# Two half projections begun one step earlier in an attention kernel's hand-written order of steps

## The chip, the cores and the metric

The kernel runs on one core of a Trainium2 chip. The metric is the device time of one execution in microseconds (us), lower is better.

## The reference

Two layers on x of 8 batches, 512 channels and 1024 positions, in float32. Only the first is touched:

```python
h = _group_norm(x, gn_w, gn_b)
qkv = jnp.einsum('oc,bcn->bon', qkv_w, h.reshape(B, C, N)) + qkv_b[None, :, None]
q, k, v = qkv.reshape(B, 3, NUM_HEADS, HEAD_DIM, N) split along axis 1
attn = softmax(jnp.einsum('bhdi,bhdj->bhij', q, k) * HEAD_DIM ** (-0.5))
out = jnp.einsum('bhij,bhdj->bhdi', attn, v)
x = x + (jnp.einsum('oc,bcn->bon', proj_w, out) + proj_b)
```

There are 8 heads of 64 channels. The second layer (a top-k attention over tokens) follows it on the same core.

## The kernel before

The first layer works through 64 heads in 32 pairs, four pairs to a batch. A head is 8 **steps**, so a pair is 16 steps, numbered 0 to 15 here; a step takes 256 keys against 512 queries. What each engine does in a step is written out by hand, and every engine runs its own list in order, waiting on semaphores.

- **PE** (`step`, L478): the second half of the weighting of an earlier step (`weigh_low`, L474, reads `p_low`); the scores, four matmuls (L447, L451); one matmul of 512 columns for the row maxima of three steps later (`take_max`, L428); then the **units** of this step; the weighting (L467, L468); a second maximum (L428). That is 12 matmuls without a unit.
- A **unit** is one half (512 positions) of a projection k, q or v of the *next* pair, a transposition of v, or a small group sum `g`. Most projections are spread: six matmuls (L372 to L374) in one step and six in the next. `PAIR_STEPS` (L52) gives, for each of the four pairs of a batch, the step in which each half begins; `parts_by_step` (L58) makes the table that all engines follow.
- **ACT** takes two exponentials of the scores, and the high part of a finished unit (L575 for q and k).
- **DVE** (`step`, L799): the reduce of the second maximum of the step before (L679); after every fourth block `row_max_top` (L687); `p_low` of the step before (L695), which frees a score tile; the reduce of this step's first maximum (L679); the low part of the units finished in the step before (L708 for q and k, two instructions); then what belongs to single steps: statistics of the next batch's x (`tile_stats`, L780 to L783, in a batch's second pair at steps 9, 11, 12 and 13), `h_low` (L787), `o_low` (L792, step 8), `reciprocal` (L797).
- **POOL** normalises a head's output (L878), when SP's transfer of the reciprocals has landed.
- **SP** issues the transfers of a step in order: copies of a finished k or q (`twins`, L938), the row of maxima (L943), the denominators (L950), weights, and in a fourth pair, at step 2, four loads of x for the residual (L980).

The maxima and units share three PSUM banks. `assign_banks` (L178) gives each one the bank that its own estimate says comes free first, and `fill_free` (L333) makes PE wait until what last had that bank has been read: by the reduce (L679) for a maximum, by the low part (L708) for q and k. So the order of units also decides which bank waits for which reduce.

Of the kernel before, what the change touches and what calls it, by code (L numbers as in the profile page):

```python
# [46 lines left out]
def begins(k0, k1, q0, q1, v0, v1, vt0, vt1, whole=()):  # L47
    begin = {("k", 0): k0, ("k", 1): k1, ("q", 0): q0, ("q", 1): q1, ("v", 0): v0, ("v", 1): v1}
    return {**{u: (s, u in whole) for u, s in begin.items()}, ("vt", 0): vt0, ("vt", 1): vt1}


PAIR_STEPS = (begins(0, 1, 6, 8, 2, 3, 3, 5, whole=(("k", 0), ("k", 1), ("v", 0), ("q", 1))),  # L52
              begins(1, 3, 5, 8, 10, 12, 12, 14),
              begins(0, 3, 6, 8, 10, 12, 12, 14),
              begins(2, 4, 6, 8, 10, 12, 12, 14))


def parts_by_step():  # L58
# [1996 lines left out]
```

## Time and profile before

| | us |
|---|---|
| median of three runs | 2720.56 |
| the three runs | 2714.07, 2722.04, 2720.56 |
| profiled execution, span | 2718.4 |
| PE busy in it | 2619.7 |
| DVE busy | 2055.1 |
| ACT busy | 1578.5 |
| POOL busy | 221.9 |

The span runs from the first to the last instruction of the profiled execution; the page gives no other time of that execution, and the time around the span is not in it. Busy time of PE is modelled at the ends of matmuls, so PE's losses are read below from start to start of the same instruction. Batches are counted from the first to the eighth; "the fifth batch" begins at 1139 us or so of the span.

### The profile page before, as it was taken

Reading aid. Unit: us, or ns where it says so; the run is one execution under the profiler, and the core shown is the slowest. Engines: PE = TensorE matmul, PEld = TensorE weight load, DVE = VectorE, ACT = ScalarE, POOL = GpSimd, SP = SyncE. Lnnn points to the kernel's source line nnn. Section 1 sums busy time; section 2 is a strip of 40 time slices with the busy share of each in tenths; the row PEclk is TensorE's granted clock in tenths of the full one; section 3 lists DMA queues with packets and bytes.
Section 4 is the critical chain, followed back from the end, with each engine's and each line's share of the span. In section 5 each row is a group of like instructions: output and inputs, shape, how many; then the busy total and the mean of one; then the engine's idle time right before and its main releaser. Section 6 shows DMA issues by size and latency. Waiting matters only on the chain.

```text
span 2718.4 us, 33180 instructions
## 1 busy us (share of the span) xinstructions
PE 2619.7 (96%) x11856; PEld 2181.7 (80%) x11856; DVE 2055.1 (76%) x3294; ACT 1578.5 (58%) x1930; POOL 221.9 (8%) x134
## 2 busy tenths in 40 slices
PE   6999999999999999999999999999999987899998
PEld 5788888888888888888888888888888876688887
DVE  6788768876887688768876887688767867878864
ACT  4667646764676467646764676567646663334311
POOL 1000000000000000000000000000000012111010
PEclk9999999999999999999999999999999999899999
DMA  4512232223222322232223222321322335466444
GB/s 156 177 50 80 67 103 61 79 71 100 64 78 67 101 67 76 63 107 67 65 72 109 66 59 79 109 67 48 90 83 58 112 127 203 171 215 246 165 164 170
DMA packets 154849, 279.48 MB, mean 103 GB/s; under 512 B 51776, under 2 KB 52032, under 8 KB 154176
## 3 DMA queue, kind: packets, MB, share of 16 engines
q1 hardware_dynamic: 152128, 268.98, 31.4%
q0 software_dynamic: 2560, 8.39, 1.0%
q8 instruction: 96, 1.57, 0.2%
q14 instruction: 65, 0.53, 0.1%
HBM read 180.04 MB, written 63.18 MB: 89 GB/s over the span
## 4 chain that ended last, share of the span: by engine, by line
PE 83%; DVE 9%; issue 3%; DMA 2%; ACT 1%; SPq 0%; POOL 0%; POOLq 0%; DVEq 0%; ACTq 0%
PE tiles L372 9%; PE tiles L373 8%; PE tiles L374 8%; PE tiles L474 8%; PE tiles L451 8%; PE tiles L428 8%; PE tiles L468 8%; PE tiles L467 8%; PE tiles L447 7%; PE tiles L1321 5%; PE tiles L1371 2%; DVE row_max L679 2%; DVE p_low L695 2%; DVE h_low L787 1%; PE tiles L383 1%
## 5 line engine op out<-in xcount | busy, mean ns | idle before, releaser
L679 DVE TENSOR_REDUCE row_max<-tiles 128x1 f32<-128x512 f32 x1014 | 694.5, 685 | 443.4 <-PE tiles L428 440.6
L544 ACT ACTIVATE p_high<-tiles 128x1024 fp32r<-128x1024 f32 x512 | 525.5, 1026 | 595.8 <-PE tiles L451 595.1
L695 DVE TENSOR_TENSOR p_low<-tiles,p_high 128x1024 fp32r<-128x1024 f32 x512 | 623.0, 1217 | 7.0 <-ACT tiles L546 6.2
L546 ACT ACTIVATE tiles<-tiles 128x1024 f32<-128x1024 f32 x512 | 523.0, 1021 | 0.0
L467 PE MATMUL tiles<-p_high,v_high 128*128 128x512 f32 x1024 | 406.5, 397 | 2.2 <-ACT num_den L562 1.5
L428 PE MATMUL tiles<-k_high_low,q_high_high 128*128 128x512 f32 x1014 | 404.8, 399 | 0.2 <-DVE row_max L679 0.2
L468 PE MATMUL tiles<-p_high,v_low 128*128 128x512 f32 x1024 | 402.0, 393 | 0.0
L428 PEld LDWEIGHTS tiles<-k_high_low,q_high_high 128*128 128x128 f32 x1014 | 312.5, 308 | 48.6 <-DVE row_max L679 5.7
L474 PE MATMUL tiles<-p_low,v_high 128*128 128x512 f32 x1024 | 325.8, 400 | 14.9 <-DVE p_low L695 14.6
L451 PE MATMUL tiles<-q_low_max,k_high_one 65*128 65x512 f32 x1024 | 325.8, 399 | 1.9 <-DMA q_low_max<-row_max_top 1.8
L372 PE MATMUL tiles<-h_high,w_high 128*128 128x512 f32 x768 | 304.6, 397 | 17.3 <-DVE row_max L679 8.3
L878 POOL TENSOR_TENSOR o_normed<-num_den,o_normed 64x1024 f32<-64x1024 f32 x64 | 153.5, 2399 | 2046.1 <-DMA o_normed<-rec_rows 2046.1
L447 PE MATMUL tiles<-q_high_high,k_high_low 128*128 128x512 f32 x1024 | 316.8, 391 | 0.0
L373 PE MATMUL tiles<-h_low,w_high 128*128 128x512 f32 x768 | 301.7, 393 | 0.0
L374 PE MATMUL tiles<-h_high,w_low 128*128 128x512 f32 x768 | 300.4, 391 | 0.0
L447 PEld LDWEIGHTS tiles<-q_high_high,k_high_low 128*128 128x128 f32 x1024 | 192.0, 188 | 47.6
L451 PEld LDWEIGHTS tiles<-q_low_max,k_high_one 65*128 65x128 f32 x1024 | 193.2, 189 | 45.6 <-DMA q_low_max<-row_max_top 4.4
L474 PEld LDWEIGHTS tiles<-p_low,v_high 128*128 128x128 f32 x1024 | 189.7, 188 | 44.9 <-DVE p_low L695 25.2
L467 PEld LDWEIGHTS tiles<-p_high,v_high 128*128 128x128 f32 x1024 | 192.5, 188 | 38.8 <-ACT num_den L562 2.3
L468 PEld LDWEIGHTS tiles<-p_high,v_low 128*128 128x128 f32 x1024 | 192.6, 188 | 38.0
L372 PEld LDWEIGHTS tiles<-h_high,w_high 128*128 128x128 f32 x768 | 145.8, 190 | 43.9 <-issue 24.2
L374 PEld LDWEIGHTS tiles<-h_high,w_low 128*128 128x128 f32 x768 | 145.1, 189 | 32.4
(167 smaller groups left out, 3138.1 us busy)
## 6 DMA issues: line engine op xcount, KB each, us to landing
x_tiles<-in_x SPq DMA_DIRECT2D x64, 512.0 KB, 5.4
w_high<-w_split SPq DMA_DIRECT2D x126, 256.0 KB, 2.8
w_low<-w_split SPq DMA_DIRECT2D x126, 256.0 KB, 3.0
k_high_one<-k_high_low SPq DMA_DIRECT2D x128, 128.0 KB, 2.3
q_high_high<-q_high_high SPq DMA_DIRECT2D x128, 128.0 KB, 2.3
o_normed<-rec_rows SPq DMA_DIRECT2D x64, 256.0 KB, 3.7
x<-x_tiles SPq DMA_DIRECT2D x32, 512.0 KB, 4.0
x_full<-x SPq DMA_DIRECT2D x32, 512.0 KB, 8.3
```

Of the source, the lines that this page charges most:

```text
L372: mm(fill[:, :], w1, high[:, c, cols], start=(c == 0), stop=False)
L374: last = mm(fill[:, :], w2, high[:, c, cols], start=False, stop=(c == CT - 1))
L428: mm(max_bank(h, i, n)[:, :], q1[:, q_slot(h), first:first + HALF - 3:4], k1[:, k_slot(h), n * HALF:(n + 1) * HALF], start=True, stop=True ...
L447: mm(out[:, n * HALF:(n + 1) * HALF], k1[:, wk, keys[n]], q1[:, wq, queries], start=True, stop=False)
L451: last = mm(out[:, n * HALF:(n + 1) * HALF], k2[0:HD + 1, wk, keys[n]], q2[0:HD + 1, wq, queries], start=False, stop=True)
L467: mm(pv[:, :], weights_of(v1, t, n), p, start=(t % 4 == 0 and n == 0), stop=False)
L468: last = mm(pv[:, :], weights_of(v2, t, n), p, start=False, stop=False)
L474: last = mm(pv[:, :], weights_of(v1, t, n), pl[:, t % 2, n * HALF:(n + 1) * HALF], start=False, stop=(t % 4 == 3 and n == 1))
L544: nc.scalar.activation(ph[:, r, :], ring[:, r, :], ACT.Exp, scale=ATT_SCALE).then_inc(s_ph, 1)
L546: nc.scalar.activation(ring[:, r, :], ring[:, r, :], ACT.Exp, scale=ATT_SCALE).then_inc(s_p32, 1)
L679: nc.vector.reduce_max(mcol[:, h % 2, n, i:i + 1], max_bank(h, i, n)[:, :], AX_X).then_inc(s_mx, 1)
L695: tt(pl[:, r, :], ring[:, r, :], ph[:, r, :].bitcast(F32), ALU.subtract).then_inc(s_pl, 1)
```

## The change

In the table for a batch's second pair, q's second half begins at step 7 instead of 8; in the fourth pair k's first half begins at step 1 instead of 2. Both are spread over two steps, so the six matmuls of step 9 (second pair) are now in step 7, and the six of step 3 (fourth pair) in step 1. The low part on DVE, the high part on ACT and the copies on SP move one step forward with them.

```diff
 PAIR_STEPS = (begins(0, 1, 6, 8, 2, 3, 3, 5, whole=(("k", 0), ("k", 1), ("v", 0), ("q", 1))),
-              begins(1, 3, 5, 8, 10, 12, 12, 14),
+              begins(1, 3, 5, 7, 10, 12, 12, 14),
               begins(0, 3, 6, 8, 10, 12, 12, 14),
-              begins(2, 4, 6, 8, 10, 12, 12, 14))
+              begins(1, 4, 6, 8, 10, 12, 12, 14))
```

The arguments of `begins` are the steps of k's two halves, q's two, v's two and the two transpositions. The seven fourth pairs that have a successor and the eight second pairs are changed.

DVE in a second pair, from the reduce of step 9's first maximum on, before (`bn_parts` and `mean_var` are the statistics of x, `q_low_max` is q's low part):

```order
L679 TENSOR_REDUCE row_max<-tiles 128x1
L780 BN_STATS bn_parts<-x_tiles 128x6 x2
L782 MEMSET carry 128x1
L783 BN_AGGR mean_var<-bn_parts 128x2
L679 TENSOR_REDUCE row_max<-tiles 128x1
L695 TENSOR_TENSOR p_low<-tiles,p_high 128x1024
L679 TENSOR_REDUCE row_max<-tiles 128x1
L708 SCALAR_TENSOR_TENSOR q_low_max<-tiles,bias_qk,q_high_high 64x512 x2
```

The same place after the change:

```order
L679 TENSOR_REDUCE row_max<-tiles 128x1
L708 SCALAR_TENSOR_TENSOR q_low_max<-tiles,bias_qk,q_high_high 64x512 x2
L780 BN_STATS bn_parts<-x_tiles 128x6 x2
L782 MEMSET carry 128x1
L783 BN_AGGR mean_var<-bn_parts 128x2
L679 TENSOR_REDUCE row_max<-tiles 128x1
L695 TENSOR_TENSOR p_low<-tiles,p_high 128x1024
```

q's low part now stands ahead of the statistics and of the reduce of step 9's second maximum.

SP in a fourth pair, around step 2 (`k_high_one` are k's copies, `q_low_max<-row_max_top` is the row of maxima):

```order
-L943 DMA q_low_max<-row_max_top 1x128x4 x2
+L943 DMA q_low_max<-row_max_top 1x128x4
+L938 DMA k_high_one<-k_high_low 64x512 x2
+L943 DMA q_low_max<-row_max_top 1x128x4
 L950 DMA den_columns<-num_den 128x1x8
 L980 DMA x_tiles<-in_x 128x1024 x4
-L938 DMA k_high_one<-k_high_low 64x512 x2
 L958 DMA rec_rows<-rec_columns 128x8
```

k's two copies stood behind the four loads of x, and now stand ahead of the row of maxima and the denominators.

PE in a third pair, at step 3, with the semaphores it waits on (`s_mx` counts reduces, `s_kql` low parts of k and q):

```order
 L451 MATMUL tiles<-q_low_max,k_high_one 128x512 x2
-L428 MATMUL tiles<-k_high_low,q_high_high 128x512 [waits s_kql]
-L372 MATMUL tiles<-h_high,w_high 128x512 [waits s_mx,s_w1]
+L428 MATMUL tiles<-k_high_low,q_high_high 128x512 [waits s_mx]
+L372 MATMUL tiles<-h_high,w_high 128x512 [waits s_kql,s_w1]
 L373 MATMUL tiles<-h_low,w_high 128x512
```

No instruction moves here; the two have exchanged their banks.

## Rows read from the trace of the kernel before

**Rows 1.** The page's busy times: engine, us, share of the span, instructions.

```profile
PE 2619.7 (96%) x11856; PEld 2181.7 (80%) x11856; DVE 2055.1 (76%) x3294; ACT 1578.5 (58%) x1930; POOL 221.9 (8%) x134
```

**Rows 2.** PE's waits over the span: waiter, releaser, us in total, times, longest.

```profile
PE tiles L474 <- DVE p_low L695: 14.6, 24, 1.7
...
PE tiles L372 <- DVE row_max L679: 8.3, 11, 1.0
```

**Rows 3.** Windows (us, busy by engine, PEclk, DMA), fifth batch: full, bare, fourth pair's 0, 1.

```profile
1249.45:1253.60 4.15, 4.15 (x20) 3.48 (x19) 3.82 (x8) 3.61 (x5) 0.00 (x0) 1.00 0.00 0
1400.72:1403.50 2.78, 2.78 (x13) 2.35 (x12) 2.75 (x5) 2.01 (x3) 0.00 (x0) 1.00 0.03 1
1339.89:1343.78 3.89, 3.38 (x13) 2.35 (x12) 3.89 (x6) 3.89 (x5) 0.00 (x0) 1.00 0.00 0
1343.78:1347.23 3.45, 3.05 (x13) 2.35 (x12) 3.45 (x5) 2.74 (x4) 0.00 (x0) 1.00 0.00 0
```

**Rows 4.** Windows, second pair's steps 7 and 8: fourth, fifth, last of eight batches, sum.

```profile
967.94:975.66 7.72, 7.46 (x32) 5.73 (x31) 7.55 (x11) 5.06 (x6) 2.40 (x1) 1.00 0.16 34
1240.96:1249.45 8.49, 7.48 (x31) 5.76 (x30) 8.30 (x11) 5.05 (x6) 1.35 (x1) 1.00 0.14 31
...
2062.93:2072.39 9.46, 7.47 (x31) 5.82 (x30) 9.29 (x11) 5.06 (x6) 2.35 (x1) 1.00 0.13 28
sum 68.74, PE 59.87 PEld 46.16 DVE 67.33 ACT 40.48 POOL 13.55; mean PE 7.48 PEld 5.77 DVE 8.42 ACT 5.06 POOL 1.69
```

**Rows 5.** Windows, fourth pair's steps 0 and 1: sum of seven batches.

```profile
sum 51.43, PE 45.05 PEld 32.88 DVE 51.43 ACT 46.38 POOL 0.00; mean PE 6.44 PEld 4.70 DVE 7.35 ACT 6.63 POOL 0.00
```

**Rows 6.** PE's timeline, fifth batch, second pair's step 8: start, us, what, [idle <-releaser].

```profile
1246.36 0.47 PE L372 MATMUL tiles<-h_high,w_high 128*128 128x512 f32 x1 [0.93 <-DVE row_max L679]
```

**Rows 7.** Line L687: ns min/median/max of one, first and last start.

```profile
L687 DVE TENSOR_TENSOR row_max_top<-row_max x128: 161/162/1917, 43.3 to 2199.1; 128x4 fp32r<-128x4 f32 x128
```

**Rows 8.** POOL's timeline, fifth batch, second pair's steps 6 and 7.

```profile
1239.92 2.40 POOL L878 TENSOR_TENSOR o_normed<-num_den,o_normed 64x1024 f32<-64x1024 f32 x1 [37.76 <-DMA o_normed<-rec_rows]
```

**Rows 9.** DVE's timeline, fifth batch, second pair's steps 7 to 9.

```profile
1241.41 0.92 DVE L687 TENSOR_TENSOR row_max_top<-row_max 128x4 fp32r<-128x4 f32 x1
...
1243.99 1.50 DVE L708 SCALAR_TENSOR_TENSOR q_low_max<-tiles,bias_qk,q_high_high 64x512 fp32r<-64x512 f32 x2
...
1247.86 1.22 DVE L792 TENSOR_TENSOR o_low<-o_normed,o_high 128x1024 fp32r<-128x1024 f32 x1
1249.18 0.69 DVE L679 TENSOR_REDUCE row_max<-tiles 128x1 f32<-128x512 f32 x1
...
1250.92 0.68 DVE L679 TENSOR_REDUCE row_max<-tiles 128x1 f32<-128x512 f32 x1
1251.52 1.28 DVE L780 BATCH_NORM_STATS2 bn_parts<-x_tiles 128x6 f32<-128x512 f32 x2
1252.84 0.20 DVE L783 BATCH_NORM_AGGREGATE mean_var<-bn_parts 128x2 f32<-128x12 f32 x1
```

**Rows 10.** PE's and DVE's timelines, fifth batch, third pair's step 3.

```profile
1289.02 0.40 PE L428 MATMUL tiles<-k_high_low,q_high_high 128*128 128x512 f32 x1
1289.52 0.47 PE L372 MATMUL tiles<-h_high,w_high 128*128 128x512 f32 x1
...
1288.68 0.69 DVE L679 TENSOR_REDUCE row_max<-tiles 128x1 f32<-128x512 f32 x1
```

**Rows 11.** DVE's timeline, fifth batch, fourth pair: last `h_low`, and step 3's reciprocal.

```profile
1347.12 1.22 DVE L787 TENSOR_TENSOR h_low<-x_tiles,h_high 128x1024 fp32r<-128x1024 f32 x1
...
1354.69 0.20 DVE L797 RECIPROCAL rec_columns<-den_columns 128x8 f32<-128x8 f32 x1 [0.92 <-DMA den_columns<-num_den]
```

**Rows 12.** SP's timeline, fifth batch: second pair's step 7, fourth pair's step 3.

```profile
1241.19 1.11 SPq L938 DMA_DIRECT2D q_high_high<-q_high_high  x2
...
1352.59 0.60 SPq L950 DMA_DIRECT2D den_columns<-num_den  x1
```

**Rows 13.** The page's transfers: KB of one, median us from issue to landing.

```profile
x_tiles<-in_x SPq DMA_DIRECT2D x64, 512.0 KB, 5.4
```

## Prediction

> **What bounds the kernel now.** I read first the page's busy shares: TensorE (PE) is busy 96% of the span, VectorE (DVE) 76% [rows 1]. So time is lost only where PE stands still, and the list of PE's own waits tells where: 14.6 us for `p_low`, which frees the score tiles, and 8.3 us for `row_max`, which frees a PSUM bank; both are DVE's work [rows 2]. Then I cut the first layer into its steps, from one pair of L447 matmuls to the next. A step holds 12 matmuls, or 18 with half a projection. A window over an undisturbed full step lasts 4.15 us, over an undisturbed bare one 2.78 us, both at granted clock 1.00 [rows 3]. What a step lasts beyond that is its loss, and the change touches two places that lose. In a second pair the bare step 7 and the full step 8 should take 6.93 us. They take 7.72 to 9.46; over eight batches 68.74 against 55.4, **13.3 us lost** [rows 4]. In a fourth pair the bare steps 0 and 1 should take 5.56 us and take 3.89 + 3.45 [rows 3]; over seven batches 51.43 against 38.9, **12.5 us** [rows 5]. All of both would be 25.8 us, 0.9% of the span; the question is what comes back where the bare step is put.
>
> All durations are from the profiled execution, whose span is 2718.4 us. Nothing gives its own time apart from the span; the median of the three runs is 2720.56, 2.2 us above the span, and I add the change to the median. A measurement here can tell about 0.3%, 8.2 us, from no change.
>
> **The second pair: no work is added, the bare step goes from 7 to 9.** I work in the fifth batch, where step 7 begins at 1240.96. Before, the half in step 8 takes the bank of the maximum that PE has just written at the end of bare step 7. Its reduce comes behind the rest of DVE's queue, and PE starts L372 only at 1246.36 [rows 6]. That goes: with a full step 7 the half uses an older bank, already read.
>
> But DVE's queue is not shortened. It opens with `row_max_top`, 0.92 us long from 1241.41, where the median of its 128 is 0.162 us [rows 7, 9]; it ends as the 2.40 us POOL operation from 1239.92 ends, at 1242.32 [rows 8]. **The Trainium skill**, "SBUF — State Buffer", section "Who interferes with whom", says that a DVE instruction with both inputs in SBUF waits for a GpSimd one that reads SBUF, and for its whole length; by that rule the trace agrees. The change moves neither operation, so the hold stays. Were nothing ever held, every batch would be like the fourth, and by the step below the sum of this place would be some 8 us in place of 4.
>
> From there DVE works without a gap to the end of `o_low` (1247.86 + 1.22 = 1249.08) [rows 9], before and after alike. After, step 9 starts at 1240.96 + 2 x 4.15 = 1249.26 and is bare; step 10 starts at 1252.05, and its half of v follows five matmuls of 0.23 us (2.78 / 12), at 1253.21. That half takes the bank of the maximum written at the end of step 9, now as before. DVE's queue in front of this reduce: the reduce of step 8 at 1249.08; step 9's first reduce 1.74 later (1249.18 to 1250.92 in the rows) at 1250.82; then, 0.60 later, q's low part, 1.50 us, which stood one step further on; then the group statistics, 1251.52 to 1253.04 in the rows, 1.52 us [rows 9]. That is 1254.44, and the awaited reduce of 0.69 us ends, overlapping a little, at 1255.1. PE starts 0.15 us behind a reduce (1288.68 + 0.69 to 1289.52 [rows 10]) and loses another 0.08 restarting: L372 at 1255.25 in place of 1253.21, **2.1 us lost where 8.49 - 6.93 = 1.56 went: +0.54**.
>
> The other batches: in the fourth, POOL's operation came late enough not to hold DVE, so only 0.79 was lost before; after, 2.05: +1.26. The last batch has no statistics: 2.53 before, DVE 0.97 later than in the fifth, so 2.1 + 0.97 - 1.52 = 1.55 after: -0.98. The five others lost 8.4 us together, their POOL operations ending from a little before to a good deal later than the fifth's; a later end raises both sides alike, an earlier one only lowers the old loss, so I take +0.6 each. Sum: 0.54 + 1.26 - 0.98 + 3.0 = **+3.8 us**. Bounds: if PE found the reduce done, -13.3; if DVE ran 0.3 us later in each batch than I set it, +6.
>
> **The fourth pair: the bare steps 0, 1 become 0, 3.** Step 0 keeps its loss of 1.11 us (3.89 - 2.78); it is `p_low` behind `v_low` and `h_low` on DVE, and neither moves. Step 1 loses its 0.67 [rows 3]: with six matmuls more PE reaches the wait after `p_low` is done. k's own inputs are there, since the last `h_low` ends at 1347.12 + 1.22 = 1348.34 [rows 11], and the matmuls that read it come in step 2, after 1349.5.
>
> New is the bare step 3, here from 1343.78 + 2 x 4.15 = 1352.08. Step 4's half of k takes the bank written at the end of step 3, and PE is at it at 1352.08 + 2.78 + 1.16 = 1356.03. DVE's queue ahead of that reduce now has k's low part (1.5 us, as q's) and the reciprocal of 0.20 us. By durations alone (reduce, top, `p_low` at 1.22, reduce, low part, reciprocal, less the overlaps, from 1351.81) the reduce ends at 1356.7: 0.9 us lost. But the reciprocal waits for the transfer of `den_columns`, and SP, in front of it, now issues k's two copies and the row of maxima. The copies begin 0.23 us into a bare step (1241.19 against 1240.96) and hold SP 1.11 us; with 0.65 for the row and the gaps, `den_columns` is issued at 1354.11. It is landed and used 2.10 us after its issue (1352.59 to 1354.69), so at 1356.21 [rows 11, 12]. Then 0.20 + 0.69 + 0.15 + 0.08, less the overlap: **1.2 us lost**. I take this end, since it goes by the same two transfers in the same queue. The row of maxima, needed at the start of step 4, may come 0.3 us late as well; that is inside the 1.2. Net 1.2 - 0.67 = +0.53, times seven: **+3.7 us** (bounds +1.6 from 0.9; -4.7 if nothing waits). The four loads of x are issued 1.5 us later; they are for residuals a pair further on, so that costs nothing.
>
> **The third pair, which the diff does not name.** The planner gives two banks the other way round: in step 3 the early maximum (L428) waits for the last reduce and k's half for an old one. Before, that reduce held L372 from 1289.25 to 1289.52 [rows 10], 0.27 us. Now it holds L428, one matmul earlier, from 1289.02 to 1289.52: 0.50. That is +0.23 in eight batches, **+1.8 us** (bounds 0 and 1.8).
>
> Sum: 3.8 + 3.7 + 1.8 = **+9.3 us**: a span of 2727.7, and 2730 on the median.
>
> **Rivals.** *The waits just go (faster).* If DVE had slack where the bare steps are put, 13.3 + 7 x 0.67 = 18.0 us would be saved: 2702.6. For it: PE's two largest waits are exactly these. It decides by one point, whether DVE reaches the reduce of step 9 before 1253.2 in the fifth batch; against it, the rows put 5.3 us of work behind 1249.08.
>
> *The swaps come out nearly even (no change).* DVE's queue as I have it, but `den_columns` lands in time, k's queue costs 0.9 us, and the banks of the third pair hide in PE's order: 3.8 + 1.6 + 0 = 5.4, so 2726. For it: the two smaller terms rest on gaps of a few tenths.
>
> *The copies of k get in the way of `den_columns` (much slower).* If its landing took 5.4 us, as the loads of x do in the median [rows 13], in place of 2.1, the fourth pair would lose 3.3 us more: 7 x 3.3 = 23, so 2753. Against it: those loads are issued behind it, now as before.
>
> **How the numbers follow.** My forecast 0.56 (own range 2726 to 2734; four fifths of it is above +8.2 us), even 0.30, just gone 0.07, copies 0.07. Slower by over 0.3%: 0.45 + 0.07 = 0.52; within 0.3%: 0.11 + 0.29 = 0.40; faster: 0.07 + 0.01 = 0.08. The range leaves out both outer rivals and takes in the runs' own spread (2714.07 to 2722.04), which moves the even case down and mine up: 2718 to 2737.
>
> **What would show it.** In the changed profile, steps 7 and 8 of a second pair last 4.15 each in most batches, step 9 2.78, and step 10 about 6.2 with L372 waiting for `row_max`; in the last batch step 10 is shorter. In a fourth pair step 0 stays at 3.89, steps 1 and 2 are 4.15, and step 4 is about 5.3, with the reciprocal waiting for its transfer just before. PE's wait for `p_low` falls by some 3 us, its wait for `row_max` grows. I am wrong if step 10 stays at 4.15 (DVE had room), or if a step outside these three pairs moves.

## The result and the profile after

The changed kernel takes 2739.96 us in the median of five runs (2733.88 to 2742.67) against 2720.56: a ratio of 1.0069, 95% interval 1.0055 to 1.0083. Slower was forecast, at 2730; it is twice as much, 19.4 us in place of 9.5, and above the range. The profiled execution is one of the shorter ones, with a span of 2733.7 us, 15.3 above the span of before.

PE's waits over the span, changed kernel (waiter, releaser, us, times, longest), against [rows 2]:

```profile
PE tiles L372 <- DVE row_max L679: 19.6, 18, 1.8
...
PE tiles L474 <- DVE p_low L695: 8.9, 14, 1.4
```

The two have changed places, in the directions forecast: PE waits less for score tiles (5.7 us less, where some 3 were forecast) and more for a bank. The time went where the steps were put. Windows over step 10 of the eight second pairs, which before lasted 4.15 us each, as the full step of [rows 3] does (columns as there: us, busy by engine, PEclk, DMA share, GB/s):

```profile
158.07:164.24 6.17, 4.41 (x20) 3.48 (x19) 4.85 (x10) 2.22 (x3) 0.00 (x0) 1.00 0.24 80
433.35:439.51 6.16, 4.40 (x19) 3.47 (x18) 4.84 (x10) 2.22 (x3) 0.00 (x0) 1.00 0.24 79
708.76:716.49 7.73, 5.97 (x19) 4.57 (x18) 4.84 (x10) 2.22 (x3) 0.00 (x0) 0.78 0.21 66
986.46:992.69 6.23, 4.41 (x20) 3.47 (x19) 4.91 (x10) 2.22 (x3) 0.00 (x0) 1.00 0.23 79
1262.19:1269.93 7.74, 5.98 (x20) 4.63 (x18) 4.84 (x10) 2.23 (x3) 0.00 (x0) 0.78 0.20 66
1539.01:1545.23 6.22, 4.40 (x19) 3.47 (x18) 4.90 (x10) 2.22 (x3) 0.00 (x0) 1.00 0.24 80
1814.31:1822.03 7.72, 5.96 (x19) 4.57 (x18) 4.97 (x10) 2.22 (x3) 0.00 (x0) 0.78 0.19 63
2092.74:2097.53 4.79, 4.40 (x19) 3.47 (x18) 3.52 (x6) 2.22 (x3) 0.00 (x0) 1.00 0.30 105
```

Four rows last what the prediction said, 6.2 us, the last 4.8. Three rows last 1.5 us more, and they alone have a granted clock below 1.00. PE's timeline in the fifth batch's step 10 (start, us, what, [idle <-releaser]):

```profile
1263.12 0.40 PE L428 MATMUL tiles<-k_high_low,q_high_high 128*128 128x512 f32 x1
1265.28 0.65 PE L372 MATMUL tiles<-h_high,w_high 128*128 128x512 f32 x1 [1.76 <-DVE row_max L679]
1265.73 0.63 PE L373 MATMUL tiles<-h_low,w_high 128*128 128x512 f32 x1
...
1268.29 0.63 PE L468 MATMUL tiles<-p_high,v_low 128*128 128x512 f32 x1
1268.72 0.45 PE L467 MATMUL tiles<-p_high,v_high 128*128 128x512 f32 x1
1269.00 0.40 PE L468 MATMUL tiles<-p_high,v_low 128*128 128x512 f32 x1
```

PE restarts 1.9 us late behind the reduce, and its next eight matmuls follow one another by 0.43 us in place of 0.23: the lower of the clock's two levels, 1.2 GHz in place of 2.4. A window over them:

```profile
1265.28:1268.72 3.44, 3.44 (x9) 2.68 (x9) 1.58 (x2) 0.00 (x0) 0.00 (x0) 0.52 0.00 0
```

The first layer of the kernel before shows no such stretch between its second step and its end. DVE's queue ahead of that wait is the forecast one; its timeline in the fifth batch's steps 9 and 10, against [rows 9]:

```profile
1259.14 0.69 DVE L679 TENSOR_REDUCE row_max<-tiles 128x1 f32<-128x512 f32 x1 [0.41 <-PE tiles L428]
...
1260.88 0.68 DVE L679 TENSOR_REDUCE row_max<-tiles 128x1 f32<-128x512 f32 x1
1261.47 1.50 DVE L708 SCALAR_TENSOR_TENSOR q_low_max<-tiles,bias_qk,q_high_high 64x512 fp32r<-64x512 f32 x2
1262.89 1.27 DVE L780 BATCH_NORM_STATS2 bn_parts<-x_tiles 128x6 f32<-128x512 f32 x2
1264.21 0.20 DVE L783 BATCH_NORM_AGGREGATE mean_var<-bn_parts 128x2 f32<-128x12 f32 x1
...
1264.44 0.69 DVE L679 TENSOR_REDUCE row_max<-tiles 128x1 f32<-128x512 f32 x1
```

By stages, from sums of windows over the same steps before and after: steps 7 to 10 of the second pairs 135.07 to 143.80 us, +8.7 (forecast +3.8); step 3 of the third pairs 36.53 to 38.51, +2.0 (+1.8); steps 0 to 4 of the fourth pairs 138.59 to 143.67, +5.1 (+3.7). Together +15.8, the span's +15.3 with small differences elsewhere. The largest of these is the first layer's very first step, 9.3 to 10.9 us; it lasts from 6.1 to 10.9 us in the nine profiled executions, whichever edit they have.

### The profile page after: what moved, and what is told of

Same layout as the page of the kernel before. It is cut to its first block, busy times and chain, and to the rows that moved or that the text cites. A ratio compares the mean times of both kernels' runs of the same rounds, so it can differ in the third digit from the quotient of the medians.

```text
span 2733.7 us, 33180 instructions
## 1 busy us (share of the span) xinstructions
PE 2626.7 (96%) x11856; PEld 2187.5 (80%) x11856; DVE 2052.3 (75%) x3294; ACT 1578.4 (58%) x1930; POOL 221.8 (8%) x134
## 4 chain that ended last, share of the span: by engine, by line
PE 79%; DVE 11%; issue 4%; DMA 3%; ACT 2%; SPq 1%; POOL 0%; POOLq 0%; DVEq 0%; ACTq 0%
PE tiles L372 8%; PE tiles L373 8%; PE tiles L374 8%; PE tiles L428 7%; PE tiles L451 7%; PE tiles L468 7%; PE tiles L467 7%; PE tiles L474 7%; PE tiles L447 7%; PE tiles L1321 5%; DVE row_max L679 3%; DVE p_low L695 2%; PE tiles L1371 2%; PE tiles L383 1%; PE tiles L1404 1%
## 5 line engine op out<-in xcount | busy, mean ns | idle before, releaser
L474 PE MATMUL tiles<-p_low,v_high 128*128 128x512 f32 x1024 | 324.7, 399 | 9.0 <-DVE p_low L695 8.9
L474 PEld LDWEIGHTS tiles<-p_low,v_high 128*128 128x128 f32 x1024 | 191.4, 188 | 35.5 <-DVE p_low L695 15.2
```

What stands on the lines that cost most here:

```text
L474: last = mm(pv[:, :], weights_of(v1, t, n), pl[:, t % 2, n * HALF:(n + 1) * HALF], start=False, stop=(t % 4 == 3 and n == 1))
```

## The experiments

My theory after the result: DVE's queue makes PE stand about two us in step 10, as forecast, and the granted clock then falls in some batches, which the forecast did not have. The rivals: the excess belongs to the other half of the edit, to the two together, or to a slower DVE or transfer, and the clock falls on its own account.

**The halves of the edit apart.** q alone:

```diff
-              begins(1, 4, 6, 8, 10, 12, 12, 14))
+              begins(2, 4, 6, 8, 10, 12, 12, 14))
```

> Only the second pair's edit (q's second half from step 7). My theory: the second pairs cost what my prediction had for them (+3.8 us) plus stretches of 3.4 us at half clock behind the wait in step 10, some 1.5 us each, in two to seven of the seven batches with statistics; the third pairs' exchanged banks add 1.7. So 9 to 16 us over the kernel before, about 2733, no loss in the fourth pairs beyond those of before. Rival (the excess comes with the fourth pairs' edit or from the two together): 5.5 us over before, about 2726, and no half-clock stretch in the first layer.

Measured: 2734.03 us in the median of five runs, 1.0056 times before (1.0036 to 1.0075). The fourth pairs are as before, and six of the seven batches with statistics have the stretch. In the third pairs the planner exchanged the banks of step 3 and of step 6 here, +3.5 us where I had 1.7. Three of the eight windows over step 10, the third, fourth and fifth batch:

```profile
708.30:716.04 7.74, 5.98 (x20) 4.69 (x19) 4.85 (x10) 2.22 (x3) 0.00 (x0) 0.78 0.20 68
985.55:991.77 6.22, 4.40 (x20) 3.47 (x18) 4.91 (x10) 2.22 (x3) 0.00 (x0) 1.00 0.23 81
1260.58:1268.31 7.73, 5.97 (x20) 4.55 (x19) 4.84 (x10) 2.22 (x3) 0.00 (x0) 0.78 0.18 64
```

k alone is the other line of the edit by itself:

```diff
-              begins(1, 3, 5, 7, 10, 12, 12, 14),
+              begins(1, 3, 5, 8, 10, 12, 12, 14),
```

> Only the fourth pair's edit (k's first half from step 1). My theory: step 4 of seven fourth pairs loses 1.4 us, step 1 no longer its 0.67: +4.7; the planner's banks may exchange in the third pairs as well, 0 to +1.8. No half-clock stretch in the first layer, since no wait of PE reaches two us. So 4.5 to 6.5 us over before, about 2726. Rival (this edit brings the excess): 10 us or more over before, with half-clock stretches.

Measured: 2725.04 us in the median of ten runs, 1.0019 (1.0010 to 1.0029) times before, which was 2719.18 on that chip: +5.9, and no stretch at the lower clock in the first layer after its first steps. Its fourth pairs lose in step 4 what the changed kernel's do (5.5 us in most; 6.7 in the fifth batch, where PE waits 1.75 us for the row of maxima), though nothing of the second pairs was touched. In the third pairs the planner exchanged the banks of step 6 here, not of step 3, which costs as much. So the excess belongs to the second pairs.

**What stands in DVE's queue.** The statistics of step 9 one step later, in the changed kernel:

```diff
-                if h % HEADS == 3 and s in (1, 3, 4, 5):
-                    tile_stats(b, (1, 3, 4, 5).index(s))
+                if h % HEADS == 3 and s in (2, 3, 4, 5):
+                    tile_stats(b, (2, 3, 4, 5).index(s))
```

> The changed kernel with DVE's first statistics of the next batch's x moved from step 9 to step 10 of a second pair, so that they no longer stand ahead of the reduce that step 10 waits for. My theory: step 10 loses 0.6 us in place of 2.0, no half-clock stretch follows it, second pairs lose some 6.5 us in all against 13.3 before; with the third and fourth pairs unchanged (+1.7, +4.7) the time is that of the kernel before, 2720, give or take 3, about 19 us under the changed one. Rival (q's low part and the hold by POOL's operation set step 10, not the statistics): step 10 still loses more than 1.5 us and the time stays above 2733.

Measured: 2718.76 us in the median of ten runs, 0.9998 (0.9988 to 1.0007) times before. Step 10 of the eight second pairs lasts 4.72 to 4.81 us, all at 1.00; the fifth batch's:

```profile
1253.95:1258.67 4.72, 4.40 (x20) 3.47 (x19) 4.63 (x10) 2.22 (x3) 0.00 (x0) 1.00 0.30 106
```

The loss there falls from 2.0 to 0.6 us, and DVE's timeline shows the awaited reduce right behind q's low part:

```profile
1253.23 1.50 DVE L708 SCALAR_TENSOR_TENSOR q_low_max<-tiles,bias_qk,q_high_high 64x512 fp32r<-64x512 f32 x2
1254.76 0.69 DVE L679 TENSOR_REDUCE row_max<-tiles 128x1 f32<-128x512 f32 x1
```

Steps 7 to 10 now sum to 129.92 against 135.07 before; they lose 8.1 us beyond undisturbed steps, where I had expected 6.5. So the statistics are 1.4 us of the wait. But this edit takes the clock's fall in step 10 away too, by taking the wait away; it does not tell whether the standing PE is what the clock answers to. One fall is left in its first layer, in the last batch's fourth pair: there PE starts L474 2.1 us late, behind `p_low`, and the clock is at 0.50 from 2188.50 to 2191.91.

**The same wait, with PE at work in it.** In step 10, where the wait is, the matmul of the first maximum is done nine times over, into the same bank with the same values:

```diff
+            if h % HEADS == 3 and h // HEADS < BATCH - 1 and i == 7 and n == 0:
+                for _ in range(8):
+                    mm(max_bank(h, i, n)[:, :], q1[:, q_slot(h), first:first + HALF - 3:4], k1[:, k_slot(h), n * HALF:(n + 1) * HALF],
+                       start=True, stop=True)
             mm(max_bank(h, i, n)[:, :], q1[:, q_slot(h), first:first + HALF - 3:4], k1[:, k_slot(h), n * HALF:(n + 1) * HALF],
```

> The changed kernel in which PE, in step 10 of the second pairs with statistics, repeats the first maximum's matmul eight times (1.84 us) ahead of the wait, writing the same values: the wait stays as long on the clock, but PE is at work in it. The product is the same, the eight matmuls are extra work. My theory (the granted clock falls because PE stands still there): step 10 still lasts 6.2 us in every batch, none lasts 7.7, no half-clock stretch in the first layer; 4 to 10 us under the changed kernel, about 2731. Rival (the clock falls for another reason, or the 7.7 us come from elsewhere): as the changed kernel, 2740, with steps of 7.7 us; if the extra matmuls come on top of the wait, 13 us over it.

Measured: 2731.10 us in the median of six runs, 1.0039 (1.0024 to 1.0054) times before, against 1.0069 (1.0055 to 1.0083) for the changed kernel. Windows over step 10, first, fifth, seventh and last batch:

```profile
160.37:166.60 6.23, 6.23 (x27) 5.35 (x26) 4.92 (x10) 2.23 (x3) 0.00 (x0) 1.00 0.25 82
...
1263.37:1269.61 6.24, 6.24 (x28) 5.35 (x27) 4.93 (x10) 2.23 (x3) 0.00 (x0) 1.00 0.25 82
...
1814.16:1820.31 6.15, 6.15 (x28) 5.35 (x27) 4.86 (x10) 2.23 (x3) 0.00 (x0) 1.00 0.25 83
2089.57:2094.29 4.72, 4.40 (x19) 3.47 (x18) 3.45 (x6) 2.23 (x3) 0.00 (x0) 1.00 0.33 106
```

PE does 1.84 us more work and the step lasts the same 6.2 us, in all seven batches, and the clock stays at 1.00. PE's timeline in the fifth batch (the added matmuls are L430, the program's own L432):

```profile
1264.30 2.04 PE L430 MATMUL tiles<-k_high_low,q_high_high 128*128 128x512 f32 x8
1266.19 0.39 PE L432 MATMUL tiles<-k_high_low,q_high_high 128*128 128x512 f32 x1
1266.53 0.47 PE L372 MATMUL tiles<-h_high,w_high 128*128 128x512 f32 x1
1266.84 0.39 PE L373 MATMUL tiles<-h_low,w_high 128*128 128x512 f32 x1
```

With the wait as long and only the standing still filled, the falls go: none in seven places, against three to six of seven in the four profiled executions where PE stands. The other five runs were not profiled; their mean granted clocks are 0.992 to 0.994, against 0.989 to 0.992 in the changed kernel's five. Steps 7 to 10 sum to 139.68 here, +4.6 against before, where the forecast had +3.8; in the changed kernel's profiled execution, with three falls, it was +8.7. So the falls are most of what the forecast left out.

**The third pairs.** The planner is held to its old banks, in the changed kernel:

```diff
         i = min(open_banks, key=lambda i: until[i])
+        if e[0] == "m" and e[1] % HEADS == 5 and e[2] in (0, 3) and e[3] == 0:
+            i = [j for j in open_banks if holder[j][0] == "k"][0]
```

> The changed kernel with the planner held to the old choice of banks in the third pairs (the maxima of steps 3 and 6 take k's bank, the halves the recent one). My theory: step 3 of the third pairs lasts 4.5 us again in place of 4.8, in all eight batches, and nothing else moves: 2 us under the changed kernel, which the runs will hardly separate, so the step lengths decide. Rival (those 0.3 us hang on something else that the change moved): step 3 stays at 4.8.

Measured: 2736.19 us in the median of four runs, 1.0052 (1.0036 to 1.0067) times before. Step 3 of the third pairs is back at 4.50 to 4.52 in six batches, and the sum over eight is 36.04 against 38.51 in the changed kernel and 36.53 before. So the +2.0 there is the exchange of banks. Its second pairs have six falls in the profiled execution.

**The fourth pairs.** SP issues k's copies behind the denominators:

```diff
+            late = h % HEADS == 6 and s == 2
             for u in here:
-                if u[0] in ("k", "q"):
+                if u[0] in ("k", "q") and not late:
                     twins(u)
...
                 if s == 2:
                     den_to_columns(h - 1)
+                for u in here:
+                    if late and u[0] in ("k", "q"):
+                        twins(u)
```

> The changed kernel with SP issuing k's two copies of the fourth pairs behind the row of maxima and the denominators, not ahead of them. My theory (the reciprocal waits there for its transfer, delayed by the copies): step 4 of the fourth pairs falls from 5.5 us to about 5.05, what DVE's queue alone costs; 3 us under the changed kernel. Rival (DVE's queue, with k's low part, sets step 4 whatever the transfer does): step 4 stays at 5.5.

Measured: step 4 lasts 5.29 to 5.31 us in place of 5.50 to 5.72, and the five steps' sum falls from 143.67 to 141.88: 1.8 us, little more than half of what was expected. The time, 2737.36 us in the median of four runs or 1.0060 (1.0044 to 1.0075) times before, can't tell 1.8 us. DVE in the fifth batch, first the changed kernel, then this one:

```profile
1366.93 1.51 DVE L708 SCALAR_TENSOR_TENSOR k_high_low<-tiles,bias_qk,k_high_low 64x512 fp32r<-64x512 f32 x2
1368.68 0.20 DVE L797 RECIPROCAL rec_columns<-den_columns 128x8 f32<-128x8 f32 x1 [0.24 <-DMA den_columns<-num_den]
1368.91 0.69 DVE L679 TENSOR_REDUCE row_max<-tiles 128x1 f32<-128x512 f32 x1
```

```profile
1369.19 1.51 DVE L708 SCALAR_TENSOR_TENSOR k_high_low<-tiles,bias_qk,k_high_low 64x512 fp32r<-64x512 f32 x2
1370.74 0.20 DVE L797 RECIPROCAL rec_columns<-den_columns 128x8 f32<-128x8 f32 x1
1370.97 0.69 DVE L679 TENSOR_REDUCE row_max<-tiles 128x1 f32<-128x512 f32 x1
```

The wait for the transfer is real, 0.24 us, but DVE's own queue alone costs 1.15 us there, not the 0.9 I had: low part, reciprocal and reduce follow each other without the small overlaps that I had taken off.

**A version that beats both.** The second pair's edit, the statistics at step 10, the old banks, and k's first half at step 2 as before (the diffs above, joined):

> What should beat both kernels: the second pair's edit, the statistics at step 10, the old banks in the third pairs, and k's first half in the fourth pairs back at step 2. My theory: the second pairs save 5 us, the third and fourth pairs are as before, no half-clock stretch in the first layer: 5 us under the kernel before, 0.2%. Rival (what the second pair saves comes back later, in the third or fourth pairs or the second layer): within 2 us of the kernel before.

Measured: 2711.97 us in the median of eight runs, against 2720.70 for the kernel before on that chip: 0.9968 (0.9958 to 0.9979). That is 8.7 us, more than the 5 expected. Between the two profiled executions its second pairs' steps 7 to 10 give 4.5 us (130.55 in sum), the third pairs about 1, and the first pairs, without their very first step, about 1. That first step is 3.2 us shorter here, but it varies by as much between executions of kernels that do not touch it, so it can't be put down to the edits; what else makes up the difference of the medians is open. No stretch at the lower clock appears in its first layer after the first steps. So q's half at step 7 gains once the statistics no longer stand where the bare step went.

## Why the prediction was wrong

- **What bounds the kernel, and where the old losses go: right.** Steps 7 and 8 are 4.15 us in most batches after, step 9 is 2.79, step 1 of the fourth pairs 4.15, step 0 stays at 3.89.
- **The second pair's new wait: right in place and length.** Step 10 loses 2.0 us behind the reduce, with q's low part and the statistics in front (forecast 2.1). The last batch, without statistics, loses 0.6 there and 1.0 in step 7: 1.6 in all, where 1.55 was forecast for step 10 alone.
- **What follows that wait: the step that failed.** The sum took the steps behind the wait at the lengths of [rows 3], "both at granted clock 1.00", and put nothing for what follows the wait, though at 2.1 us the new wait was longer than any for `p_low` or `row_max` before (1.7 us at most, [rows 2]). The runs show the clock at its lower level for 3.4 us behind such a wait, 1.5 us lost each time: three times in the profiled execution of the changed kernel, six, six and five times in those of q alone, the kept banks and the denominators first, never when PE was kept at work. That is the missing term: 3 x 1.5 = 4.5 us in the profiled execution. In the medians the changed kernel is 19.4 us above before and the kernel with PE kept at work 11.9, so the term is some 7.5 us there, an estimate across two sets of runs, of the 10.1 us by which the forecast of +9.3 was exceeded. The changed kernel's mean granted clocks are 0.992 and 0.991 in the two shortest (spans 2732.0 and 2733.7), and 0.989 in the three others (2738.1 to 2740.8). How many falls each of those had is not seen, since only one was profiled.
- **Banks inside the second pair: a smaller omission.** I said that in a full step 7 "the half uses an older bank, already read". That holds, but the second maximum of step 7 now takes the bank of the first, and where POOL holds DVE long it waits for that reduce; the fourth batch, hardly held in the profile of before, shows it in the changed kernel's timelines of DVE, POOL and PE (start, us, what):

```profile
974.91 1.91 DVE L687 TENSOR_TENSOR row_max_top<-row_max 128x4 fp32r<-128x4 f32 x1
...
974.41 2.39 POOL L878 TENSOR_TENSOR o_normed<-num_den,o_normed 64x1024 f32<-64x1024 f32 x1 [38.19 <-DMA o_normed<-rec_rows]
...
978.61 0.62 PE L428 MATMUL tiles<-k_high_low,q_high_high 128*128 128x512 f32 x1 [0.54 <-DVE row_max L679]
```

  The first two rows end together, at 976.82 and 976.80. By the rule of the Trainium skill on "SBUF — State Buffer", section "Who interferes with whom" (a VectorE operation with both inputs in SBUF waits out a GpSimd one that reads SBUF), the trace agrees here too. Which batches are held differs between the profiled executions. With the falls taken out, the second pairs come to +4.6 us against my +3.8 (steps 7 to 10 with PE kept at work).
- **The third pairs: right**, +2.0 for +1.8, and shown by holding the banks. Step 6 stayed as it was.
- **The fourth pairs: right in mechanism, too small.** Step 4 lost 1.38 us, not 1.2, so +5.1 and not +3.7; of it the transfer's wait is 0.24 us and DVE's queue 1.15. The overlap that the sum subtracted at its end did not occur. In the seventh batch the row of maxima came 0.8 us late, not 0.3, and step 4 lasts 5.72. The copies delayed `den_columns` by no more than the sum had (the reciprocal starts 4.15 us behind the start of step 3, forecast 4.13), so the rival of slow copies fell.
- The rival that the waits just go fell at the point named for it: in the fifth batch DVE reached the reduce of step 9 1.1 us after PE stood at the half of v, and ended it 1.8 us after. That the swaps come out even fell with it.
- Without the falls my terms come to 4.6 + 2.0 + 5.1 = 11.7 us where I had 9.3; the kernel with PE kept at work gives 11.9 above before. That would have been inside the range.

## What to carry to other kernels

A bare step given to PE is a debt on the engine that feeds it: before moving one, list what the feeding engine has queued at the new place, statistics and other occasional work included, and move that work away in the same edit. Price a wait of PE by its length and by what the granted clock does behind it; that second price came on top here, and was paid in only some of the places. And where a planner gives out banks, read its answer anew in the stages that the edit does not touch.

## What the runs showed of the hardware

- A wait of PE of two us, in a stretch of otherwise steady matmuls, is followed in some cases by 3.4 us at the lower clock level. In four kernels with this wait it was 3, 6, 6 and 5 of seven batches. In all four the fourth batch had none, at the same length of wait; why it is spared was not tried. The length of the wait alone does not decide: of two waits for `p_low` at the same place of the last batch, one that made PE start 2.1 us late was followed by a fall (statistics moved) and one of 2.2 us was not (q alone). In step 4 of the fourth pairs PE starts 0.9 to 1.1 us late in most batches, and no fall follows in these profiles.
  With the statistics moved: PE's timeline (start, us, what) and a window over the fall; then PE's timeline with q alone. (Late is counted from the start that 0.23 us behind the matmul before would give; the idle time in brackets is a little less.)

```profile
2186.98 0.73 PE L474 MATMUL tiles<-p_low,v_high 128*128 128x512 f32 x2 [1.93 <-DVE p_low L695]
...
2188.50:2191.91 3.41, 3.41 (x10) 2.63 (x10) 3.38 (x7) 3.23 (x4) 0.00 (x0) 0.50 0.02 1
```

```profile
2200.69 0.73 PE L474 MATMUL tiles<-p_low,v_high 128*128 128x512 f32 x2 [2.07 <-DVE p_low L695]
```

- Eight further matmuls in the wait cost nothing and kept the clock: 6.15 to 6.24 us a step with them, 6.16 to 7.74 in the changed kernel without, over the seven batches with statistics.
